# Weights of projections and folded heads loaded one stage ahead, kept rows stored one stage later, attention's results stored by SyncE

## The reference, cut to what matters

```python
def _gat(x, src, dst, W, a_src, a_dst, b, heads, out_ch, concat):
    h = (x @ W).reshape(n, heads, out_ch)
    al_s, al_d = einsum('nhc,hc->nh', h, a_src), einsum('nhc,hc->nh', h, a_dst)
    e = leaky_relu(al_s[src] + al_d[dst], 0.2)
    alpha = segment softmax of e over dst
    out = segment_sum(h[src] * alpha[:, :, None], dst)
    ...
h = elu(_gat(x, ..., W1, ..., heads=4, out_ch=128, concat=True))    # g1
h = elu(_gat(h, ..., W2, ..., heads=4, out_ch=128, concat=True))    # g2
h = _gat(h, ..., W3, ..., heads=1, out_ch=256, concat=False)        # g3
...
q, k, v = split(einsum('bnd,ed->bne', x, w_qkv))                     # 8 heads of 64
dots = einsum('bhnd,bhne->bhde', instance_norm(k), instance_norm(v))
out = einsum('bhnd,bhde->bhne', q, dots) / N;  mix = out @ w_out.T + b_out
x = x + gat_mlp(xn) + mix
```

## Time and profile before

| what | value |
|---|---|
| median of 3 runs | 3723.67 us (3722.82 to 3724.9) |
| profiled execution | 3723.46 us |
| its span on the core | 3722.0 us |
| PE busy | 3261.3 us (88%) |
| DVE busy | 2070.4 us (56%) |
| ACT busy | 1707.3 us (46%) |
| POOL busy | 232.3 us (6%) |
| DMA, HBM traffic | mean 114 GB/s |
| g1a matmuls (L1904) | 5200, 574.9 us |
| g2a matmuls (L1904) | 5200, 575.2 us |

### The profile page before, as it was taken

One profiled execution on the slowest core, in us unless ns is written; L12 is line 12 of the kernel. 1 busy time (PEld: TensorE's weight loads), 2 busy tenths in 40 slices (PEclk: granted clock), 3 DMA queues, 4 the chain that ended last, 5 costly groups with the idle time before them and its releaser, 6 DMA issues. The chain is left out here.

```text
span 3722.0 us, 75746 instructions
## 1 busy us (share of the span) xinstructions
PE 3261.3 (88%) x32397; PEld 2992.8 (80%) x32397; DVE 2070.4 (56%) x2243; ACT 1707.3 (46%) x2005; POOL 232.3 (6%) x320
## 2 busy tenths in 40 slices
PE   3788877878469999687999999699999997999899
PEld 3568877878469998356899999679999996999676
DVE  6665558989542221653566767326767762666411
ACT  0534457878233333230555555225655552555332
POOL 1000000000012222002000100100001001000000
PEclk9879989999579999798999999899999998999889
DMA  3223345433246554301655655325656544544020
GB/s 113 51 45 51 52 85 130 119 89 88 80 169 210 185 185 144 71 12 43 160 152 155 174 140 151 85 69 159 165 143 175 146 126 129 159 136 127 6 59 27
DMA packets 176755, 424.91 MB, mean 114 GB/s; under 512 B 72469, under 2 KB 104990, under 8 KB 175052
## 3 DMA queue, kind: packets, MB, share of 16 engines
q1 hardware_dynamic: 159134, 383.68, 38.2%
q0 software_dynamic: 13904, 33.84, 3.0%
q10 hardware_dynamic: 3399, 2.76, 0.3%
HBM read 366.69 MB, written 53.50 MB: 113 GB/s over the span
## 5 line engine op out<-in xcount | busy, mean ns | idle before, releaser
L1904 PE MATMUL g2a_ps<-HX,g2a_x 125*125 125x129 f32 (+2 forms) x5200 | 575.2, 273 | 3.4 <-ACT g2a_grow L1858 3.3
L1904 PE MATMUL g1a_ps<-HX,g1a_x 125*125 125x129 f32 (+2 forms) x5200 | 574.9, 273 | 3.4 <-ACT g1a_grow L1858 3.4
L1904 PEld LDWEIGHTS g2a_ps<-HX,g2a_x 125*125 125x125 f32 x5200 | 574.8, 189 | 3.7 <-ACT g2a_grow L1858 3.5
L1904 PEld LDWEIGHTS g1a_ps<-HX,g1a_x 125*125 125x125 f32 x5200 | 574.6, 188 | 3.8 <-ACT g1a_grow L1858 3.6
L1755 DVE SCALAR_TENSOR_TENSOR g2a_x<-g2a_x,g2a_flat,g2a_ct 125x3125 f32<-125x3125 f32 (+2 forms) x104 | 348.2, 3350 | 183.0 <-ACT g2a_x L1812 171.4
L1755 DVE SCALAR_TENSOR_TENSOR g1a_x<-g1a_x,g1a_flat,g1a_ct 125x3125 f32<-125x3125 f32 (+2 forms) x104 | 348.2, 3350 | 182.7 <-ACT g1a_x L1812 174.3
L1812 ACT ACTIVATE g2a_x<-g2a_grow,g2a_near,g2a_steep 125x3125 f32<-125x3125 f32 (+2 forms) x104 | 300.9, 2897 | 243.1 <-PE g2a_ps L1904 242.8
L1812 ACT ACTIVATE g1a_x<-g1a_grow,g1a_near,g1a_steep 125x3125 f32<-125x3125 f32 (+2 forms) x104 | 300.9, 2897 | 242.9 <-PE g1a_ps L1904 242.6
L1904 PE MATMUL g0a_ps<-HX,g0a_x 125*64 125x65 f32 (+1 forms) x10000 | 318.1, 228 | 84.7 <-DVE g0a_x L1755 44.4
L1904 PEld LDWEIGHTS g0a_ps<-HX,g0a_x 125*64 125x64 f32 (+1 forms) x10000 | 309.8, 142 | 93.1 <-issue 45.6
L1755 DVE SCALAR_TENSOR_TENSOR g0a_x<-g0a_x,g0a_flat,HX 125x3125 f32<-125x3125 f32 (+2 forms) x104 | 341.4, 3346 | 31.4 <-ACT g0a_x L1812 31.2
(11 more groups left out here) (579 smaller groups left out, 3920.5 us busy)
## 6 DMA issues: line engine op xcount, KB each, us to landing
HX<-counted SPq DMA_DIRECT2D x100, 683.6 KB
g1a_ct<-counted SPq DMA_DIRECT2D x100, 683.6 KB
g2a_ct<-counted SPq DMA_DIRECT2D x100, 683.6 KB
moe_wa<-in_L_ffn_W SPq DMA_DIRECT2D x56, 1024.0 KB
counted<-HX SPq DMA_DIRECT2D x12, 1367.2 KB
HX<-counted SPq DMA_DIRECT2D x100, 79.3 KB
g1a_ct<-counted SPq DMA_DIRECT2D x100, 79.3 KB
g2a_ct<-counted SPq DMA_DIRECT2D x100, 79.3 KB
```

The source lines that it names most:

```text
L1904: return nc.tensor.matmul(ps[64 * j:64 * j + b - a, c, col:col + f1 - f0], x[:, (step * J + j) % XR, t * R + a:t * R + b], HX[:, sb, gr * ...
```

## The change

1. wq and wo become tiles that live across lina and linb; SyncE loads them in lina, after lina's own loads. linb only waits for their semaphore.
2. A helper `layer` makes the tiles of a projection's weights and bias outside the stage and returns them with the list of their loads. g1p's are loaded by SyncE in lo, g2p's by SyncE in g1a, g3p's in g2a, one transfer in each of the iterations m = 10 and on. The projection stages get them as `ready` and issue none themselves.
3. lo no longer stores X. g1p's SyncE stores it whole, in one `tile_dma`, and waits for it at its end.
4. In g1a and g2a SyncE stores the chunks instead of GpSimd. Those of group gr go out in the loop over count tiles, chunk c in iteration m = CR + 5 + 25 (gr + 1) + c, after that iteration's wait and count tile; those of the last group go out after the loop.

The diff, with context cut:

```diff
-def stage_gat_project(nc, m, g, feed, KC, w, att_s, att_d, bias, AL, HX, kept=None, ahead=None, folds=None):
+def stage_gat_project(nc, m, g, feed, KC, w, att_s, att_d, bias, AL, HX, keep=None, ahead=None, folds=None, ready=None):
...
     with Stage(nc, g.name + "p") as s:
-        if kept is not None:
-            s.sems.append(kept)
-        wt = s.sb("w", [P, KC, PARTS, WP + SC])
+        if keep is not None:
+            s.sems.append(keep[2])
+        if ready is None:
+            wt, bt = s.sb("w", [P, KC, PARTS, WP + SC]), s.sb("bt", [R, HF])
+            loaded, bias_in = s.sem("loaded"), s.sem("bias_in")
+        else:
+            wt, bt, loaded, bias_in = ready
+            s.sems.extend([loaded, bias_in])
...
             att, prod = s.sb("att", [P, 2, HF]), s.sb("prod", [P, 2, HF])
-        bt = s.sb("bt", [R, HF])
...
         ps = s.ps("ps", 3 * PARTS)
-        loaded, folded, bias_in = s.sem("loaded"), s.sem("folded"), s.sem("bias_in")
+        folded = s.sem("folded")
...
                 tile_dma(sp, *ahead)
-            if kept is not None:
-                sp.wait_ge(kept, 32 * T)
+            if keep is not None:
+                tile_dma(sp, *keep)
+                sp.wait_ge(keep[2], 32)
...
             act.sem_inc(h_free, 2)
-            if folds is not None:
+            if folds is not None and ready is None:
...
-def stage_gat_sums(nc, m, g, AL, HX, OUT, X=None, spare=None, ct_out=()):
+def stage_gat_sums(nc, m, g, AL, HX, OUT, X=None, spare=None, ct_out=(), ahead=()):
...
+        def store(sp, gr, c):
+            n, t0, t1 = gr * CH + c, tiles[c][0], tiles[c][-1] + 1
+            sp.wait_ge(y_ready, n + 1)
+            tile_dma(sp, OUT[t0 * R:t1 * R, gr * F:(gr + 1) * F].rearrange("(t p) f -> p t f", p=R), y[:, n % YR, 0:t1 - t0, :], y_out[n % YR])
...
                 tile_dma(sp, ct[:, m_ % CR, :], m.CT[sb * R:(sb + 1) * R], ct_in[m_ % CR])
+                if 0 <= m_ - 10 < len(ahead):
+                    dst, src, sem = ahead[m_ - 10]
+                    sp.dma_start(dst, src).then_inc(sem, 16)
+                gr, c = (m_ - CR - 5) // T - 1, (m_ - CR - 5) % T
+                if g.out == "elu" and gr >= 0 and c < CH:
+                    store(sp, gr, c)
+            if g.out == "elu":
+                for c in range(CH):
+                    store(sp, GR - 1, c)
+                for k in range(YR):
+                    sp.wait_ge(y_out[k], 32 * (G * CH // YR))
...
             nc.gpsimd.memset(under[:], UNDER).then_inc(stepped, 1)
-            if g.out == "elu":
-                for n in range(G * CH):
-                    gr, c = n // CH, n % CH
-                    t0, t1 = tiles[c][0], tiles[c][-1] + 1
-                    pool.wait_ge(y_ready, n + 1)
-                    tile_dma(pool, OUT[t0 * R:t1 * R, gr * F:(gr + 1) * F].rearrange("(t p) f -> p t f", p=R), y[:, n % YR, 0:t1 - t0, :], y_out[n % YR])
-                for k in range(YR):
-                    pool.wait_ge(y_out[k], 32 * (G * CH // YR))
...
         DOTS = cc.enter_context(nc.sbuf_tensor("lin_DOTS" + Names.tag, [P, PAIRS, P], F32))[:]
+        wq, wo = [cc.enter_context(nc.sbuf_tensor(f"lin_{n}" + Names.tag, [P, PAIRS, D], F32)) for n in ("wq", "wo")]
+        heads_in = nc.alloc_semaphore("lin_heads_in" + Names.tag)
...
                     sp.dma_start(rows[:, j, :], v.partition_broadcast(R)).then_inc(rows_in, 16)
+                sp.dma_start(wq[:], a["w_q"].rearrange("(c p) n -> p c n", p=P)).then_inc(heads_in, 16)
+                sp.dma_start(wo[:], a["w_outT"].rearrange("(c p) n -> p c n", p=P)).then_inc(heads_in, 16)
...
         with Stage(nc, "linb") as s:
-            wq, wo = s.sb("wq", [P, PAIRS, D]), s.sb("wo", [P, PAIRS, D])
+            s.sems.append(heads_in)
...
             ps, psw = s.ps("ps", PAIRS), s.ps("psw", 2)
-            loaded, full, moved, done = s.sem("loaded"), s.sem("full"), s.sem("moved"), s.sem("done")
+            full, moved, done = s.sem("full"), s.sem("moved"), s.sem("done")
...
-            @block.sync
-            def _(sp):
-                sp.dma_start(wq[:], a["w_q"].rearrange("(c p) n -> p c n", p=P)).then_inc(loaded, 16)
-                sp.dma_start(wo[:], a["w_outT"].rearrange("(c p) n -> p c n", p=P)).then_inc(loaded, 16)
...
             def _(pe):
-                pe.wait_ge(loaded, 32)
+                pe.wait_ge(heads_in, 32)
...
-def stage_rows_add(nc, m, name, parts, X, KEEP=None, kept=None):
+def stage_rows_add(nc, m, name, parts, X, ahead=()):
...
                 sp.dma_start(wt[:], w.rearrange("(c p) n -> p c n", p=P)).then_inc(loaded, 16)
-            if KEEP is not None:
-                with sp.Fori(0, T // U) as i:
-                    for k in range(U):
-                        t = i * U + k
-                        wait_apart(sp, s.tick, rp.free[0], t + 3)
-                        tile_dma(sp, KEEP[:, ds(t, 1)].rearrange("p o d -> p (o d)"), cols(X[:, ds(t, 1), :]), kept)
+            for dst, src, sem in ahead:
+                sp.dma_start(dst, src).then_inc(sem, 16)
...
-            def attention(g, OUT, X=None, spare=None, ct_out=()):
+            def layer(g, KC, c):
...
+                if general:
+                    return None, ()
+                parts = max(g.heads * g.feat // 256, 1)
+                cols, scores = g.heads * g.feat // parts, 2 * g.heads // parts
+                wt, bt = sb(f"{g.name}_w", [P, KC, parts, cols + scores], F32, c), sb(f"{g.name}_bt", [R, g.heads * g.feat], F32, c)
+                loaded, bias_in = [nc.alloc_semaphore(f"{g.name}_{n}" + Names.tag) for n in ("w_in", "bias_in")]
+                w, bias = a[f"L1_gnn_W{g.name[1]}"], a[f"L1_gnn_b{g.name[1]}"]
+                loads = [(wt[:, k, :, 0:cols], w[k * P:(k + 1) * P].rearrange("p (x n) -> p x n", x=parts), loaded) for k in range(KC)]
+                return (wt, bt, loaded, bias_in), loads + [(bt[:], bias.partition_broadcast(R), bias_in)]
...
+            def attention(g, OUT, X=None, spare=None, ct_out=(), ahead=()):
...
                 else:
-                    stage_gat_sums(nc, m, g, AL, rows_of(g), OUT, X, spare, ct_out)
+                    stage_gat_sums(nc, m, g, AL, rows_of(g), OUT, X, spare, ct_out, ahead)
...
                     kept = nc.alloc_semaphore("rows_kept" + Names.tag)
-                    stage_rows_add(nc, m, "lo", [(XT, 2, WEFF)], X, m.XS, kept)
-                    stage_gat_project(nc, m, g1, XT, 2, a["L1_gnn_W1"], a["L1_gnn_a_src1"], a["L1_gnn_a_dst1"], a["L1_gnn_b1"], AL, rows_of(g1), kept, None, WA[1])
-            attention(g1, m.Y)
-            stage_gat_project(nc, m, g2, m.Y, 4, a["L1_gnn_W2"], a["L1_gnn_a_src2"], a["L1_gnn_a_dst2"], a["L1_gnn_b2"], AL, rows_of(g2), None, None, WA[2])
-            attention(g2, m.Y)
+                    ready, loads = layer(g1, 2, c)
+                    stage_rows_add(nc, m, "lo", [(XT, 2, WEFF)], X, loads)
+                    stage_gat_project(nc, m, g1, XT, 2, a["L1_gnn_W1"], a["L1_gnn_a_src1"], a["L1_gnn_a_dst1"], a["L1_gnn_b1"], AL, rows_of(g1), (m.XS, X, kept), None, WA[1], ready)
             with ExitStack() as c:
+                ready, loads = layer(g2, 4, c)
+                attention(g1, m.Y, ahead=loads)
+                stage_gat_project(nc, m, g2, m.Y, 4, a["L1_gnn_W2"], a["L1_gnn_a_src2"], a["L1_gnn_a_dst2"], a["L1_gnn_b2"], AL, rows_of(g2), None, None, WA[2], ready)
+            with ExitStack() as c:
+                ready, loads = layer(g3, 4, c)
+                attention(g2, m.Y, ahead=loads)
...
                 x_back = nc.alloc_semaphore("x_back" + Names.tag)
-                stage_gat_project(nc, m, g3, m.Y, 4, a["L1_gnn_W3"], a["L1_gnn_a_src3"], a["L1_gnn_a_dst3"], a["L1_gnn_b3"], AL, rows_of(g3), None, (X, m.XS, x_back), WA[3])
+                stage_gat_project(nc, m, g3, m.Y, 4, a["L1_gnn_W3"], a["L1_gnn_a_src3"], a["L1_gnn_a_dst3"], a["L1_gnn_b3"], AL, rows_of(g3), None, (X, m.XS, x_back), WA[3], ready)
...
                     attention(g3, Y, None, ROWS[0:R, T * 258:T * 258 + 2 * N])

```

## The result

The changed kernel takes 3781.44 us (3778.39 to 3790.68), the kernel before 3723.67 (3718.41 to 3724.9), both medians of 5 runs. The ratio is 1.0168 [1.0153, 1.0183] (in brackets the 95% interval, which stays above 1): 1.7% slower. The forecast was 3746 with a range of 3700 to 3785, so the time lies inside the range, at its upper end.

A forecast was written before the change was run, and what follows sets the result against it. Stages closed by barriers cost their slowest chain plus the border, with TensorE bounding g1a and g2a. 3723.5 less 50.1 us of border gains plus 73 of store waits gave 3746 us, range 3700 to 3785.

The forecast's parts named there:

- The borders: Stage borders from lina to g3p: loads ahead and moved stores gain 50.1 us in all, bounds 41 to 57.
- The clock in front of g1p: Start of g1p: a gap of 2.1 us might keep TensorE's clock up; half of 4.6 slow us, 2.3, counted as gain.
- Rival D: Borders: the change doesn't do what it says at one, 10 to 20 us less gain, 3756 to 3766; chance 0.06.
- The mechanism: g1a, g2a: VectorE's division waits for SyncE's late store, 24 times, 4 to 5 us each, holding TensorE; loss 73 us.
- rival A: g1a, g2a: the store slips past the count tile, L about 3, loss 15, time 3689, faster; chance 0.18.
- C: g1a, g2a: L between 4.1 and 4.7, gains and stalls cancel, 3716 to 3730; chance 0.12.
- L: g1a, g2a: time from a weighing's end to the store's landing, taken as 5.4 us, bounds 2.5 to 6.9.
- the forecast's formula: g1a, g2a: all six groups lose 24 L - 57 us; with the gains, the change is worth 24 L - 107.
- the upper bound of 6.9: g1a, g2a: L if the count tile's traffic (4.8 us) passes first, then the shortest store seen (2.1).
- rival B: g1a, g2a: longer queueing, L = 6.5, costs 99 us, slow clock after gaps 12 more: 3784; chance 0.14.
- +22.5: Whole kernel: the forecast's net change in us, a loss of 73 inside the attentions less 50.1 gained at borders.
- the Trainium skill's rule: g1a, g2a: one queue's descriptors go in order, so the moved store starts behind the whole count tile; strictly held, 3782.

The follow-up runs named there:

- moving the store: Changed kernel with SyncE sending each chunk's store one or two steps earlier: 3669.46 and 3670.81 us; issued ahead of the count tile in the same iteration: 3686.75 us.
- part 4 alone: The kernel before with only the SyncE chunk stores of g1a and g2a put in, nothing loaded ahead, X stored in lo: 3823.39 us, ratio 1.0279.

## Why the prediction was right on the sign and wrong on the size

**The borders.** Each step gave what it was to give within 1.1 us: lina and linb 6.3 (5.5 forecast; linb alone gave 7.2, and lina took 0.8 more, which the forecast had priced at nothing to 1), lo 10.7 (9.6), g1p 9.8 (9.3), ends 12.0 (13.0), g2p 9.3 (8.5), g3p 4.9 (4.2). The clock in front of g1p stayed up, as half expected. Rival D is out.

**The mechanism.** Twelve waits a stage, on the stores' DMA, VectorE in front of TensorE, none in group 3, all as forecast. Undoing part 4, moving the store, and more buffers each take the loss away, and part 4 alone brings it. Rivals A and C are out: L is neither 3 nor 4.5 (C's times are 3715 to 3729 by the forecast's formula, not 3716 to 3730, which changes nothing). Weighings 30 to 34 of g1a start 12.5, 10.5, 10.9 and 11.7 us apart, where 9.9 was forecast.

**The failed step is the value of L, 5.4 us.** It was read from the earlier trace rows as the time at which the DMA ran dry in cycles with count tile and store, 5.9 and 5.2 us after a weighing. Three things were wrong in that. First, traffic that ends is not a store that has landed: in the 24 cycles 0.6 us lie between the two in the mean, and that was left out. Second, 5.4 lies under the mean of the two rows, 5.55, with VectorE's stall as the reason. No run shows that a stall shortens L: with VectorE stalled the traffic ended 6.1 us after the weighing in the mean (7.0 in the firsts of the foursomes, 5.8 in the others), later than in the two rows. Third, the nearest row was another. The DMA view of the kernel before has GpSimd's second store DMA, of the 13 last partitions, by itself (name, count, KB each, median us from issue to landing):

```profile
attended<-g1a_y POOLq DMA_DIRECT2D x28, 168.0 KB, 4.2
...
attended<-g1a_y POOLq DMA_DIRECT2D x28, 19.5 KB, 5.0
```

A division waits for both DMAs. The small one takes the longer, 5.0 us, and with 1.5 us from a weighing to its issue it gives 6.5. It can even be read in one of the two cycles of the earlier trace rows, the one whose weighing ends at 1960.06 and whose traffic ends at 1966.0. The DMA view from 1961.5 to 1963 has, for that store:

```profile
q1 hardware_dynamic: 82, 0.49, 94.3%
q0 software_dynamic: 1, 0.00, 0.0%
...
attended<-g1a_y POOLq DMA_DIRECT2D x1, 19.5 KB, 5.1
```

Issued at 1961.52, it landed 5.1 us later, 6.6 after the weighing and not 5.9. And the forecast's sentence that in these cycles GpSimd's store was moved while the count tile was doesn't hold for the tile's main part: from 1961.5 to 1963 next to nothing passed on GpSimd's queue (q0). The store waited behind most of the tile in the kernel before as well; it only left two steps earlier. I quoted the median over both DMAs, 4.3, and only against rival A. The measured mean is 6.7, next to the upper bound of 6.9.

By the forecast's own formula L = 6.7 costs 24 x 6.7 - 57 = 104 us, 31 more than 73. The other 10 or so of the 114.5 fit rival B's price for the clock, 12 us. The matmuls of g1a and g2a are 42 us longer, with the granted clock at half in 19 of the 24 cycles, and where VectorE waits again most of that lies within its wait. Behind the last wait of a foursome nothing hides it. The first and the last restart of g1a's first foursome:

```profile
1942.81 7.64 PE L1917 MATMUL g1a_ps<-HX,g1a_x 125*125 125x129 f32 x52 [1.99 <-DVE g1a_x L1768]
...
1975.78 9.48 PE L1917 MATMUL g1a_ps<-HX,g1a_x 125*125 125x129 f32 x60 [4.03 <-DVE g1a_x L1768]
```

Behind the last restarts of the six foursomes the clock is at half for 5.4, 3.4, 0, 6.0, 6.0 and 3.4 us in the trace, and half of that is lost, 12 us. So rival B, at 0.14, was the case that happened. It took L = 6.5 and gave 3784; its time on the median of runs is 3781. Gaps of over 4 us, which it had in each cycle, came in five of the 24 (2.9 us in the mean of g1a's); the slow matmuls fill part of them.

**The rest of the difference** between +22.5 and +67 is 5.4 us in stages that the change doesn't touch (g0a +3.3, the feed-forward part +2.1), less 2.9 us that the borders gave beyond the forecast. The profiled execution was also 9 us over the median of its kernel; the runs as a whole are +57.8.

**The rule on queues.** The prediction said that if the Trainium skill's rule held strictly, the kernel would be at 3782. That is the time measured, and half of the reason holds: the moved store does start behind most of the count tile. But it lost no turns by the move, since a late store from GpSimd's own queue waits as long. What it lost is the two steps by which it used to leave earlier. The number was luck, and the run that told the two reasons apart was the one with the late store from the other queue.

## What to carry to other kernels

Read the landing of a transfer where it is measured, for each DMA of it apart, and take the slowest of those that a semaphore counts; the moment when traffic ends is earlier. When a store moves to an engine whose loop waits for the step that needs its buffer, count in steps where it leaves and where it must have landed: here one step earlier, or four more buffers, turns 1.7% slower into 1.3% faster. And what can be issued before a bulk load in the same iteration should be: the load's traffic was two thirds of the time from the weighing to the landing.

## What the runs showed of the hardware that I had not expected

- GpSimd holds up a stage's end for some 6 us after its last DMAs, though they have landed: 10.2 to 10.5 us from VectorE's end to the next stage with its stores (before and with part 4 undone), 3.8 to 4.7 with SyncE's, and 3.9 when its last DMA was 99 us old. In the kernel before the last store of g1a landed at 2370.1 and the next stage began at 2376.53. Why it holds it up was not looked into.
- The length of a gap alone doesn't tell whether TensorE's clock falls. After 1.86 us (linb), 2.09 (lo), 2.39 (g1p) and 2.02 (at 2300.23 in g1a) it ran on at full clock. After 1.99 us (at 1942.81) and 2.81 (at 1953.26) it was at half within a microsecond, and 52 matmuls took 7.64 us in place of 5.72.
- A store issued right behind a count tile starts when most of the tile is through (first traffic 3.2 to 4.2 us after the weighing) and lands after it, from SyncE's queue or from GpSimd's (6.7 us after the weighing in the mean), while one just ahead of it lands in 2.3, where no other load is under way.
